# The low parts of the experts' activations: which engine subtracts them

## What is computed

```python
def _moe(x, rw, rb, w1, b1, w2, b2):           # T = 2048 tokens, D = 128, FF = 512, E = 8, K = 2
    T = x.shape[0] * x.shape[1]
    xf = x.reshape(T, D)
    router_weights = jax.nn.softmax(xf @ rw + rb, axis=-1)
    topw, topi = jax.lax.top_k(router_weights, K)
    topw = jax.nn.softmax(topw, axis=-1)
    combine = jnp.zeros((T, E), xf.dtype).at[jnp.arange(T)[:, None], topi].add(topw)
    h = jax.nn.gelu(jnp.einsum('td,edf->etf', xf, w1) + b1[:, None, :], approximate=False)
    eo = jnp.einsum('etf,efd->etd', h, w2) + b2[:, None, :]
    out = jnp.einsum('etd,te->td', eo, combine)
    return out.reshape(x.shape)
```

## Time and profile before

| | us |
|---|---|
| median of three runs | 975.99 |
| lowest, highest | 975.27, 978.34 |
| the profiled execution | 975.2 |
| span of its instructions | 973.3 |
| its granted TensorE clock, mean over the span | 0.945 of 2.4 GHz |

### The profile page before, as it was taken

One profiled execution on the slowest core, in us unless ns is written; L12 is line 12 of the kernel. 1 busy time (PEld: TensorE's weight loads), 2 busy tenths in 40 slices (PEclk: granted clock), 3 DMA queues, 4 the chain that ended last, 5 costly groups with the idle time before them and its releaser, 6 DMA issues.

```text
span 973.3 us, 23678 instructions
## 1 busy us (share of the span) xinstructions
PE 853.8 (88%) x8603; PEld 521.1 (54%) x8603; DVE 718.1 (74%) x1555; ACT 644.6 (66%) x1583; POOL 550.1 (57%) x1074
## 2 busy tenths in 40 slices
PE   4988888876665889999899899999889989999996
PEld 1444444443333456555666456555556557776775
DVE  5788889778885666576458667767747887979776
ACT  1899999958886314544356455655546588898985
POOL 2788888856663435763345555656425354646533
PEclk9999999876775999999999799999999999999999
DMA  8500000000000000000000010000000000000000
GB/s 267 181 1 2 0 0 1 2 1 1 1 1 0 1 0 1 2 2 2 1 2 2 20 25 25 22 24 25 3 1 3 2 1 2 2 7 7 7 7 22
DMA packets 23580, 16.48 MB, mean 17 GB/s; under 512 B 8745, under 2 KB 20401, under 8 KB 23345
## 3 DMA queue, kind: packets, MB, share of 16 engines
q1 hardware_dynamic: 23472, 15.06, 5.4%
HBM read 10.85 MB, written 1.05 MB: 12 GB/s over the span
## 4 chain that ended last, share of the span: by engine, by line
PE 60%; DVE 18%; ACT 13%; issue 5%; POOL 2%; DMA 0%; SPq 0%; DVEq 0%; ACTq 0%; POOLq 0%
ACT sb_E L1284 10%; PE ps_context L806 6%; PE ps_context L809 4%; PE ps_scores L906 4%; PE ps_scores L882 4%; PE ps_turned L1184 2%; PE ps_turned L1185 2%; PE ps_turned L1186 2%; PE ps_scores L1163 2%; PE ps_scores L1161 2%; PE ps_scores L1162 2%; PE ps_scores L759 2%; PE ps_turned L720 2%; PE ps_scores L799 2%; PE ps_turned L1121 2%
## 5 line engine op out<-in xcount | busy, mean ns | idle before, releaser
L1284 ACT ACTIVATE sb_E<-ps_scores,sb_neg_max,sb_score_scale 128x256 f32<-128x256 f32 (+1 forms) x384 | 190.9, 515 | 21.9 <-DVE sb_neg_max L1585 16.1
L2346 POOL TENSOR_SCALAR sb_E<-sb_E,sb_inv_sum 128x256 f16<-128x256 f32 x256 | 123.6, 483 | 27.4 <-DVE sb_inv_sum L1621 7.6
L1794 DVE TENSOR_REDUCE sb_neg_half<-ps_scores 128x16 f32<-128x1024 f32 x48 | 58.7, 1223 | 63.6 <-PE ps_scores L882 63.6
L1539 ACT ACTIVATE sb_E<-ps_scores,sb_ff_bias 128x512 f32<-128x512 f32 x128 | 88.7, 693 | 22.1 <-PE ps_scores L1163 17.1
L1604 DVE TENSOR_REDUCE sb_neg_quad<-ps_scores 128x2 f32<-128x512 f32 (+1 forms) x96 | 64.4, 685 | 42.5 <-PE ps_scores L761 30.4
L720 PE MATMUL ps_turned<-sb_ident 128*128 128x512 f16 x289 | 86.8, 420 | 9.6 <-DVE sb_ident_b L2217 9.6
L1312 ACT ACTIVATE sb_E<-ps_scores 128x512 f32<-128x512 f32 x96 | 57.1, 598 | 48.6 <-PE ps_scores L801 47.3
L1411 ACT ACTIVATE sb_E<-ps_scores 128x1024 f32<-128x1024 f32 x48 | 49.1, 1023 | 54.8 <-PE ps_scores L914 54.8
L1580 DVE TENSOR_REDUCE sb_neg_raw<-ps_scores 128x4 f32<-128x1024 f32 x64 | 77.9, 1217 | 7.1 <-PE ps_scores L692 7.0
L1284 ACT ACTIVATION_READ_ACCUMULATOR sb_E<-ps_scores,sb_neg_max,sb_score_scale 128x1 f32 x384 | 80.0, 208 | 0.0
L2279 POOL TENSOR_SCALAR sb_veps<-sb_mv 128x2 f32<-128x2 f32 x72 | 18.3, 255 | 99.8 <-DVE sb_mv L1562 99.0
(11 more groups left out here) (315 smaller groups left out, 2593.5 us busy)
## 6 DMA issues: line engine op xcount, KB each, us to landing
sb_moe_up<-in_moe_up SPq DMA_DIRECT2D x1, 2048.0 KB
sb_KS<-sb_qk_parts SPq DMA_DIRECT2D x96, 16.0 KB, 1.8
sb_QS<-sb_qk_parts SPq DMA_DIRECT2D x96, 16.0 KB, 1.8
sb_rows<-in_rows SPq DMA_DIRECT2D x1, 1216.0 KB, 7.2
out_x<-sb_raw_context SPq DMA_DIRECT2D x8, 128.0 KB, 1.8
sb_X<-in_x SPq DMA_DIRECT2D x1, 768.0 KB, 9.3
sb_square<-in_square SPq DMA_DIRECT2D x1, 768.0 KB, 10.7
sb_ctxT<-in_ctxT SPq DMA_DIRECT2D x1, 512.0 KB, 11.1
```

What stands on the lines that cost most here:

```text
L1284: last = act.activation(E[:, ring, head], SC[t % 2][:, head], ACT.Exp, bias=neg_max[:, ring, h:h + 1], scale=scale, accum_out=row_sum[:, r ...
L1539: act.activation(U_full[:, n % RING, :], banks[n % 4], ACT.Gelu, bias=bias, scale=1 / WEIGHT_SCALE)
L1794: dve.tensor_reduce(neg_half[:, n % 2, :, :, :].rearrange("p x i g -> p (x i g)"), SC[0][:, :].rearrange("p (h k) -> p h k", k=CTX), AX.X, ...
L2346: last = pool.tensor_scalar(E16[:, ring, SEQ * h:SEQ * h + SEQ], E[:, ring, SEQ * h:SEQ * h + SEQ], inv_sum[:, ring, h:h + 1], HALF, ALU.m ...
```

## The change

One line. The list of tiles whose low part GpSimd subtracts becomes empty:

```diff
@@ -269,7 +269,7 @@
 EXP1_AT, EXP2_AT, FIRST_EXP2 = 23, 31, 7
 ROUTER_AT, TURN_AT, BIAS_AT = 22, 8, 14
 FIRST_TURN, FIRST_BIAS = 14, 20
-BY_POOL = [n for n in range(128) if n % 4 == 3 and n not in (3, 27, 59, 91)]
+BY_POOL = []
 STEPS = ["q1", "k1", "v1", "w1", "q2", "k2", "v2", "w2"]
```

## The result

Seven runs of the changed kernel have a median of 970.81 us (966.43 to 973.31), the kernel before 976.24 in seven runs beside them (975.27 to 978.42): ratio 0.9938, 95% interval 0.9914 to 0.9963. By the medians that is 5.4 us less (by the ratio 6.1), where 2.0 were forecast, and outside the range that began at 971.5. A second comparison, shown further down, gave 0.9966 (0.9953 to 0.9980), 3.8 us less by the medians and 3.3 by the ratio.

The account below looks back on a forecast made before the run. TensorE was taken to set the experts' stage's pace, with some 6 us lost behind VectorE within reach. Terms -0.6 + 0 - 0.8 - 0.5 - 0.1 = -2.0 us from a median of 975.99 gave 974.0 us, range 971.5 to 977.5.

Parts of the forecast that it names:

- Chunk 0: Experts' first chunk: split 6 comes 0.87 us earlier, the first take 0.55 us earlier; -0.6 us.
- One of the signs named ahead: Chunk 0: TensorE's waits for the first take and for split 6 shorter by 0.6 to 0.9 us in sum each.
- Chunk 1's border: No idle TensorE row there; two added splits cost 1.22 us, one lock returns about 0.9; 0, bounds -0.2 and +0.3.
- Chunk 2's border: Released locks end the wait for split 66, a smaller one for split 67 appears; -0.8 us.
- The new wait for split 67: Chunk 2's border: added split 67 ends after TensorE wants that tile; a wait of 0.5 us.
- Chunk 3's border: Repeats chunk 2's border with a smaller loss, 0.46 + 0.16 us, nearly all given back; -0.5 us.
- The end: Last split before the last down-matmuls: VectorE does it 0.5 us faster than GpSimd; -0.1 us, bounds -0.5 and +0.6.
- 0.8 us of overlap: TensorE's five waits for VectorE: each costs 0.16 us beyond its idle time, 0.8 us together.
- some tenths: Experts' stage: time lost where TensorE is just late without an idle row, counted in a whole of some 6 us.
- No gain at the borders: Rival, chance 0.20: locks given back and splits added cancel also in chunks 2 and 3; about 975.5 us.
- All of VectorE's waits go: Rival, chance 0.10: the relief reaches further than counted, -6 us, 970.0 us.
- The slow rival: Chance 0.12: locks hardly come back, added splits make VectorE late at the borders; +4.3 us, 980.3 us.

Follow-up runs that it names:

- second comparison: The kernel before and the changed kernel, each once more with nothing edited, on one chip: medians 974.72 and 972.30 us, changed kernel's ratio 0.9966.
- dummy_read: Changed kernel, with GpSimd doing an unused subtraction of the same size at the 28 old places: 981.78 us median, ratio 1.0069.
- k23: Changed kernel, but the splits of tiles 23, 55 and 87 stay with GpSimd: 973.13 us in its one run.
- after_again: The changed kernel once more, nothing edited: 972.30 us median, ratio 0.9966 against the kernel before.
- border: Against the kernel before, VectorE takes over only the 11 splits at chunk borders; GpSimd keeps the other 17: 973.70 us median, ratio 0.9980.

## Why the prediction was wrong

**The sign and the mechanism were right.** GpSimd's subtractions held VectorE's instructions with two SBUF inputs, and this relief outweighs 28 splits more; dummy_read and k23 show it from two sides. TensorE, ScalarE and SyncE behaved as their unchanged programs suggested.

**The range was wrong by the part of the program that the change doesn't touch.** I set the range from the stage's costs and three runs of the kernel before, and gave the 778 us ahead no scatter beyond theirs. Of the 5.4 us of the first comparison, 2.9 are the stretch's. In the profiled execution the stretch also began 4.2 us early, with another granted clock ahead of it, which after_again did not show again; that the clock makes up the other 2.5 us of the medians is inferred from this, not measured run by run. Three of the seven runs, at 966.4 to 967.8, have a mean clock of 0.952 to 0.957, the other four 0.945 to 0.947. So it was ill luck that the median fell under 971.5: the second comparison's, 972.30, lies within the range. The size was too small all the same. Against the second comparison, 0.9953 to 0.9980, a forecast of 974.0 (0.9980 of 975.99) stands at the edge, and its 2.0 us are two thirds of the stretch's 2.9.

**The terms, by steps:**

- Chunk 0, -0.6: measured -0.7. The wait for split 6 fell by the 0.87 us forecast. The take came 0.66 us earlier, where 0.55 was worked out. One of the signs named ahead was wrong: TensorE's wait for the first take was to become shorter, and it grew by 0.21 us, because the wait for split 6 ahead of it shrank by more than the take gained.
- Chunk 1's border, 0: measured -0.2. TensorE had lost some time here without an idle row; the bound of -0.2 was this.
- Chunk 2's border, -0.8: measured -1.1. From split 60 to split 66 VectorE gained 10.79 - 10.17 = 0.62 us, where 0.61 was worked out. The new wait for split 67 makes TensorE 0.65 us late (0.49 of them idle), where 0.51 was worked out. What was missing is loss of the kernel before that no idle row shows: down-matmul 64 had started 1.54 us behind 63, not 1.32, and that 0.22 went too (rows below the list). And I took the time from tile 67 to 68 as 1.92 us, which was 1.76 once nothing waited: I subtracted the idle 0.64 us, but not the 0.16 that a wait costs beyond its idle time, as I had said myself.
- Chunk 3's border, -0.5: measured -0.8. It had no new wait, since no further chunk follows and no statistics stand there behind tile k = 2; I had taken it as a smaller copy of chunk 2's border. All of the old loss went: the 0.62 us that I had named, and 0.21 at tile 96 that no idle row shows.
- The end, -0.1: measured -0.1. From the last gelu's end to the last tile's down-matmul it is 1.21 us in place of 1.29, by the timelines, and the take behind the split came in time.

The starts of down-matmuls 63 and 64 in the kernel before, with no idle time shown:

```profile
875.32 0.22 PE L1184 MATMUL ps_turned<-sb_moe_down,sb_KBD 128*128 128x128 f16 x1
...
876.86 0.22 PE L1184 MATMUL ps_turned<-sb_moe_down,sb_E 128*128 128x128 f16 x1
```

So the step of the sum that failed is **the size of what TensorE lost at the three borders**: the terms 0, -0.8 and -0.5 measured -0.2, -1.1 and -0.8. I named 0.8 us of overlap and "some tenths" without an idle row, but left those tenths out of the terms, where they belonged with the waits: 0.2, 0.22 and 0.21 us at the borders of chunks 1, 2 and 3.

**The rivals.** "No gain at the borders" is out by border. "All of VectorE's waits go" gave the nearest time, 970.0 for 970.81, by luck, and is wrong as a cause: 2.7 us of the waits are still there. The slow rival is answered by dummy_read: when the locks come back on top of the splits, the kernel is slower than the one before by 0.7%. Its rule, in the Trainium skill's page Perfetto Trace Analysis, section Optimizing Scalar/DVE Operations, to take work off a full VectorE, holds here in its second half: between these two engines it did not help (2.9 us of the stretch lost).

**What stays open** is why the granted clock ahead of the experts differs between executions of one program, and whether that could be steered. No kernel here tried it. Open too is why the power holds no split, and what the locks of dummy_read cost apart from the splits. k23 has one run; its reading rests on the rows and the stretch.

## What to carry to other kernels

Work given to GpSimd to relieve VectorE was paid for by VectorE here where a split or a tiny step with two SBUF inputs met a long GpSimd instruction that reads SBUF: look at VectorE's tiny instructions beside GpSimd's, and count the stretching against the work saved. Where GpSimd has to work, place its instructions in a part in which VectorE has slack; moving one pair of them, three times over, brought 1.8 us in the old kernel, where taking away the eleven subtractions at the borders brought 1.9. And compare a stage with itself (first to last instruction, here 0.02 us apart in two profiles of each kernel) before a difference of whole runs is given to a change.

## What the runs showed of the hardware

- A split that starts 0.04 us behind a GpSimd instruction reading SBUF waits for nearly all of it: it lasts 1.24 us beside one of 0.73, and 1.65 beside one of 1.15, for 0.69 undisturbed. It ends 0.55 and 0.54 us behind the other's end. A GpSimd fill that only writes, 0.95 us long, leaves two splits at 1.28 us together, but a tensor_scalar of 128x4 beside a fill lasted 0.33 and 0.44 us for 0.16.
- GpSimd's power of 128x32 elements lasts 5.43 us, and splits that start within it last 0.68 and 0.69 us.
- An order of starts that differs by some hundredths decides who is held: with L2479 ahead of the split, the split takes 1.24 us; in the changed kernel GpSimd's instructions of the same kind, L2479 and L2482, when they start 0.03 or 0.04 us behind a split, last 1.25 and 1.24 us, and the split takes 0.69.
- Executions of the same program began this stage between 777.39 and 777.82 us (the kernel before) or 773.65 and 777.43 (the changed one), with the granted clock high and low at other moments, while the stage itself, at a clock of 1.00, repeats to 0.02 us (187.24 and 187.26; 184.36 and 184.37).
